# Four score-table units ahead of the sort products, and half of the keyed one-hot rows made by ScalarE

## The reference, cut to what matters

```python
x1 = x[edges[0]]
x2 = x[edges[1]]
e = jnp.concatenate([x1, x2], axis=1) @ Ww + bw          # 12288 x 1024
e = e.reshape(-1, H, 2 * HD).transpose(1, 0, 2)
e = jax.nn.leaky_relu(e, 0.01)
w = (e @ Wa + ba)[..., 0]
mat = jnp.full((H, n, n), -jnp.inf, jnp.float32)
mat = mat.at[:, edges[0], edges[1]].set(w)
mat = jnp.nan_to_num(jax.nn.softmax(mat, axis=-1))
y = jnp.matmul(mat, out).transpose(1, 0, 2)
```

## Time and profile before

| | us |
|---|---|
| three runs | 1829.89, 1833.54, 1833.86 |
| their median | 1833.54 |
| the profiled execution | 1831.71 |
| its span, from the first to the last instruction | 1829.8 |

### The profile page before, as it was taken

The page is one execution under the profiler, slowest core; times in us unless marked ns, Lnnn a source line. Parts: engine busy times, 40 slices in busy tenths (PEclk is TensorE's granted clock), DMA queues, the critical chain, the costliest instruction groups (busy, mean ns, idle before and its releaser), DMA issues.

```text
span 1829.8 us, 22981 instructions
## 1 busy us (share of the span) xinstructions
PE 1593.3 (87%) x7110; PEld 879.4 (48%) x7111; DVE 920.3 (50%) x2224; ACT 501.2 (27%) x1607; POOL 521.8 (29%) x548
## 2 busy tenths in 40 slices
PE   5989999997697999999993396769699899999698
PEld 3534444445444646455552273624244455555455
DVE  8888888887644343443443035988732101011322
ACT  1134444447421414132230112511210211111233
POOL 5843333333332332222233721637500000000000
PEclk9999999998798999999996597679899999999899
DMA  7030101005424233232213472656525222210020
GB/s 307 6 102 20 57 24 59 24 8 131 121 56 129 63 88 79 59 105 56 70 47 93 117 259 70 176 145 185 166 69 189 69 75 69 97 53 28 8 62 18
DMA packets 132571, 162.74 MB, mean 89 GB/s; under 512 B 62041, under 2 KB 74601, under 8 KB 132114
## 3 DMA queue, kind: packets, MB, share of 16 engines
q1 hardware_dynamic: 105888, 116.45, 20.6%
q0 software_dynamic: 18752, 29.91, 6.3%
q10 hardware_dynamic: 7858, 15.44, 2.6%
HBM read 145.87 MB, written 15.88 MB: 88 GB/s over the span
## 4 chain that ended last, share of the span: by engine, by line
PE 64%; DMA 16%; DVE 12%; issue 5%; ACT 2%; POOL 1%; DVEq 0%; ACTq 0%; POOLq 0%; SPq 0%
PE psum L377 62%; DMA tab_sorted<-rec,pos 12%; DVE arena L2572 2%; DMA tab_w<-xT,pair 1%; DVE ring L1329 1%; DVE stats L468 1%; DMA ring<-tab_h,sd_t 1%; DVE ring L1264 1%; PE psum L1008 1%; DMA arena<-tab_h,sd_t 0%; PE psum L2231 0%; DMA arena<-tab_w 0%; DVE arena L1332 0%; DVE arena L1238 0%; DVE ring L1236 0%
## 5 line engine op out<-in xcount | busy, mean ns | idle before, releaser
L377 PE MATMUL psum<-arena 128*128 128x24 bf16 (+8 forms) x2026 | 324.0, 317 | 30.2 <-DVE arena L654 12.9
L377 PE MATMUL psum<-arena,ring 128*128 (+1 forms) x1504 | 327.3, 364 | 8.8 <-issue 6.3
L377 PE MATMUL psum<-xT,ring 128*128 128x384 f32 x928 | 318.6, 505 | 10.0 <-ACT ring L3006 4.2
L377 PE MATMUL psum<-ring,arena 128*128 128x512 f32 (+1 forms) x592 | 271.4, 605 | 8.7 <-DVE ring L654 3.9
L377 PEld LDWEIGHTS psum<-arena 128*128 128x128 bf16 (+5 forms) x2026 | 198.6, 149 | 162.0 <-issue 74.1
L377 PE MATMUL psum<-ring,xT 128*128 128x512 f32 x552 | 251.1, 607 | 2.5 <-DMA bc<-in_wide 1.4
L377 PEld LDWEIGHTS psum<-xT,ring 128*128 128x128 f32 x928 | 182.1, 198 | 140.2 <-issue 29.1
L377 PEld LDWEIGHTS psum<-arena,ring 128*128 128x128 bf16 (+1 forms) x1504 | 140.2, 115 | 127.4 <-issue 28.4
L1059 ACT ACTIVATE ring<-ring 128x128 f32<-128x128 f32 x416 | 123.3, 298 | 179.8 <-DVE ring L1329 179.8
L2114 POOL DMA_INDIRECT tab_sorted<-rec,pos x104 | 100.0, 961 | 237.2 <-DMA tab_sorted<-rec,pos 224.6
L377 PEld LDWEIGHTS psum<-ring,arena 128*128 128x128 f32 (+1 forms) x592 | 102.6, 187 | 135.3 <-issue 134.2
(11 more groups left out here) (455 smaller groups left out, 1600.1 us busy)
## 6 DMA issues: line engine op xcount, KB each, us to landing
ring<-in_L_ffn_w SPq DMA_DIRECT2D x22, 1024.0 KB, 8.0
ring<-in_L_gnn_m_w SPq DMA_DIRECT2D x8, 1024.0 KB, 5.9
ring<-in_L_ffn_expert_weights SPq DMA_DIRECT2D x8, 1024.0 KB, 5.3
ring<-tab_key ACTq DMA_DIRECT2D x24, 256.0 KB, 3.2
ring<-in_L_gnn_Wv SPq DMA_DIRECT2D x5, 1024.0 KB, 5.1
tab_w<-xn SPq DMA_DIRECT2D x6, 768.0 KB, 15.1
ring<-in_L_gnn_Ww SPq DMA_DIRECT2D x4, 1024.0 KB, 17.3
ring<-in_L_gnn_wq SPq DMA_DIRECT2D x4, 1024.0 KB, 5.6
```

What stands on the lines that cost most here:

```text
L377: return nc.tensor.matmul(o, a, b, start=start, stop=stop)
```

## The change

`EARLY` becomes 4, so units 0 to 3 stand ahead of the first group, and `AFTER_GROUP` gives out units 4 to 9 after groups 2, 4, 5, 7, 8 and 10, so that none follows group 11. Of the eight keyed rows of a group, ScalarE makes the first four in two activations each: the distance from the place, `abs(r - n)`, into a new tile `apart`, and `relu(key - key * distance)` into `spread`, which is the key where the distance is 0 and nothing elsewhere. VectorE makes the other four and the eighth column one-hot as before, and one new small instruction for the negated keys. TensorE waits for ScalarE's half too (`act_spread`). ScalarE's unit parts are now placed after the groups by the list that VectorE has. The gathers of the third block use eight `rows_landed` semaphores of their own.

```diff
-        rows_landed = sems("rows_landed", GR - UN) + ranks_landed
+        rows_landed = sems("rows_landed", UN)
...
         def row_landed(eng, T):
-            earlier = 1 if T % GR < 2 * NT else RECORDS + ST // UN if T % GR >= GR - UN else 0
-            eng.wait_ge(rows_landed[T % GR], 16 * (earlier + T // GR + 1))
+            earlier = 1 if T % UN < 2 * NT else 0
+            eng.wait_ge(rows_landed[T % UN], 16 * (earlier + T // UN + 1))
...
+        ACT_SPREADS = UN // 2
+        key_less = cs_e
+        apart = view(e0, 2, ACT_SPREADS, P)
...
-        EARLY = 2
-        AFTER_GROUP = {1: 2, 2: 3, 4: 4, 5: 5, 7: 6, 8: 7, 10: 8, 11: 9}
+        EARLY = 4
+        AFTER_GROUP = {2: 4, 4: 5, 5: 6, 7: 7, 8: 8, 10: 9}
         SPLIT_AFTER = {0: 0, 1: 1, 3: 2, 4: 3, 6: 4, 7: 5, 9: 6, 10: 7, 11: 8}
...
-            unit(0)
-            unit(1)
+            for u in range(EARLY):
+                unit(u)
...
                 pe.wait_ge(spread_made, g + 1)
+                pe.wait_ge(act_spread, g + 1)
...
             top_part(0)
-            for u in range(len(UNITS)):
+            act.wait_ge(keys_ready, 1)
+            for g in range(ET // UN):
+                if g >= 2:
+                    act.wait_ge(sort_used, g - 1)
+                for j in range(ACT_SPREADS):
+                    t = UN * g + j
+                    last = nc.scalar.activation(apart[:, g % 2, j, :], iota[:, 0:P], ACT.Abs, bias=r_f[:, t:t + 1], scale=-1.0)
+                last.then_inc(apart_made, 1)
+                act.wait_ge(apart_made, g + 1)
+                for j in range(ACT_SPREADS):
+                    t = UN * g + j
+                    last = nc.scalar.activation(spread[:, g % 2, j, :], apart[:, g % 2, j, :], ACT.Relu, bias=slo1[:, t:t + 1],
+                                                scale=key_less[:, t:t + 1])
+                last.then_inc(act_spread, 1)
+                if g in SPLIT_AFTER:
+                    middle_part(SPLIT_AFTER[g])
+            for u in range(len(SPLIT_AFTER), len(UNITS)):
+                middle_part(u)
...
+            V.tensor_scalar(key_less, slo1, -1.0, None, ALU.mult).then_inc(keys_ready, 1)
...
-                    last = V.tensor_scalar(spread[:, g % 2, j, :], iota[:, 0:P], r_f[:, t:t + 1], slo1[:, t:t + 1],
-                                           ALU.is_equal, ALU.mult)
+                    if j >= ACT_SPREADS:
+                        last = V.tensor_scalar(spread[:, g % 2, j, :], iota[:, 0:P], r_f[:, t:t + 1], slo1[:, t:t + 1],
+                                               ALU.is_equal, ALU.mult)
```

More of the change, by code:

```diff
@@ L266, in gnn_ffn_program @@
         spread_made = sem("spread_made")
+        apart_made = sem("apart_made")
+        act_spread = sem("act_spread")
         sort_used = sem("sort_used")
@@ L276, in gnn_ffn_program @@
         hote_made = sem("hote_made")
+        keys_ready = sem("keys_ready")
         z_full = sem("z_full")
@@ L638, in pool_scatter_rows @@
                     row_landed(pool, T - ROWS_UNDERWAY)
-                pool_gather(go_rows[T % GR], table, sd_t[:, T:T + 1]).then_inc(rows_landed[T % GR], 16)
+                pool_gather(go_rows[T % GR], table, sd_t[:, T:T + 1]).then_inc(rows_landed[T % UN], 16)
         def dve_scatter_rows(dve, od):
@@ L1039, in top_part, with middle_part @@
                 nc.scalar.activation(unit_part(u, 0), b, ACT.Copy).then_inc(hi_made, 1)
-            top_part(0)
-            for u in range(len(UNITS)):
+            def middle_part(u):
                 if u + 1 < len(UNITS):
@@ L1046, in _ @@
                 nc.scalar.activation(unit_part(u, 1), left_f[:, u % 2, :], ACT.Copy).then_inc(bf16_made, 1)
+            top_part(0)
+            act.wait_ge(keys_ready, 1)
[16 more added lines that the diff above has]
+                middle_part(u)
             act.wait_ge(sorted_cleared, 16)
@@ L1262, in _ @@
                     if j >= POOLED:
-                        V.tensor_scalar(slot_one[:, g % 2, j, :], iota[:, 0:P], q_f[:, t:t + 1], None, ALU.is_equal)
-                    last = V.tensor_scalar(spread[:, g % 2, j, :], iota[:, 0:P], r_f[:, t:t + 1], slo1[:, t:t + 1],
-                                           ALU.is_equal, ALU.mult)
+                        last = V.tensor_scalar(slot_one[:, g % 2, j, :], iota[:, 0:P], q_f[:, t:t + 1], None, ALU.is_equal)
+                    if j >= ACT_SPREADS:
+                        last = V.tensor_scalar(spread[:, g % 2, j, :], iota[:, 0:P], r_f[:, t:t + 1], slo1[:, t:t + 1],
+                                               ALU.is_equal, ALU.mult)
                 last.then_inc(spread_made, 1)
```

## The result

The changed kernel takes 1836.62 us (median of 22 runs, 1831.33 to 1842.01), the kernel before 1830.57 us in 22 runs beside them (1825.07 to 1838.0): a ratio of 1.003, interval 1.0019 to 1.004. It is 0.3% slower, where "no difference" was forecast. The profiled execution of the changed kernel is the 1842.01 us one, with a span of 1840.3 us; the pair of traces is 10.5 us apart, the medians 6.05 us. So the traces show where time goes, and the ratios how much it usually is.

What follows compares the result with a forecast made beforehand. TensorE was taken to bound the stage's second half, so unit 11's end counted: 97.4 or 99.4 us against 98.4, middle 0.0, hence 1833.5 us beside the runs' median of 1833.54. The range ran from 1829 to 1838.

Steps and rivals of the forecast that it cites:

- B: Sort stage: GpSimd isn't late, its rows get quicker as VectorE sheds work; -4.5 us, 1829.0 us; chance 8%.
- C: Sort stage: ScalarE becomes the maker TensorE waits for; unit 11 7.3 us later, 1840.8 us; chance 10%.
- I take the middle, 0.0: End of unit 11: between -1.0 and +1.0 us against 98.4 us, the change was put at 0.0.
- Case D: Sort stage: exchange of waits with slow GpSimd groups and low clock behind the keys; +2.7 us, 1836.2 us; chance 22%.
- the low clock behind the keys: Units 10 and 11: the wait for the keys might lower TensorE's clock, costing 1.7 us, at even chances.
- the slow bound of 4.25 to 4.90: GpSimd's one-hots in groups 2 to 4: 4.25 or 4.90 us a group, the slow value being 4.90.
- healing: GpSimd's slow groups: half the row work on VectorE might make them quicker; nothing showed whether it would.
- hidden, but for 0.4 us: Group 2: a low clock of 3.41 us would be covered by the 1.3 us wait for group 4.
- the 99.4 of the bad end: End of unit 11 with GpSimd's slow groups: 99.4 us, +1.0 us against 98.4.
- It has slack to catch up: GpSimd's record and weight scatters: starting 1 to 3 us later costs nothing, given 19 waits of 35.6 us in all.
- those 1 to 3 us: GpSimd's scatters: the cost if it had no slack to catch up after its later group 11.
- an exchange of waits: Sort stage, the main forecast: old waits go, new ones come; -1.0 to +1.0 us, 1833.5 us; chance 60%.

Runs made afterwards that it cites:

- run 3: The kernel before with only the eight own semaphores for the gathers of the third block: 1887.21 us, ratio 1.001.
- run 4: The changed kernel as it is, profiled a second time, against the kernel before: 1888.4 us, ratio 1.0025.
- run 5: The kernel before with only the new order of units (four early); VectorE makes all eight keyed rows: 1893.2 us, ratio 1.0039.
- run 2: The kernel before with unit 11 computed twice on TensorE, GpSimd's order untouched: 1888.93 us, ratio 1.003.
- run 8: As run 6, with GpSimd making five of a group's column one-hots instead of seven and VectorE three; against the kernel before: 1887.63 us, ratio 1.0013.
- run 9: The kernel before with 24 instead of 20 record scatters ahead of the weight scatters: 1884.91 us, ratio 0.9971.
- run 10: The kernel before without GpSimd's one-hots in the last two groups and with 24 record scatters ahead: 1893.9 us, ratio 1.003.
- run 6: The changed kernel with the old unit order, ScalarE's rows kept and its unit parts moved; against the kernel before: 1887.39 us, ratio 1.0001.
- run 11: run 8 without GpSimd's one-hots in the last two groups and with 26 record scatters ahead; against the kernel before: 1892.05 us, ratio 1.0025.
- run 1: The kernel before with seven unused one-hots chained on GpSimd behind its last group: 1893.08 us, ratio 1.005.
- run 12: run 8 with 24 instead of 20 record scatters ahead; against the kernel before: 1834.51 us, ratio 0.9995.
- run 7: The kernel before with the 76 late record scatters issued between the weight scatters: 1893.77 us, ratio 1.0029.

## Why the prediction was wrong

**What held.** TensorE went to group 0 at 34.9 us (34.4 forecast), the wait of 1.80 us went, GpSimd became the late maker with a standstill of 5.2 us, and the keys cost 2.2 us (2.4) once unit 9 no longer covered them. ScalarE's group is 2.9 us for 3.0 forecast, no table was loaded, VectorE and ScalarE were late for no group: rivals B and C are out. No cost of the semaphores shows (run 3). The Trainium skill, "ScalarE: Activation LUTs", section "What ACT_TABLE_LOAD costs", would have given ScalarE's price closer than my rows of other shapes: a start of 186 ns with 0.833 ns a column, 93 ns for each operand that is a column of SBUF, 93 ns of overlap. Worked out for 128 columns, as an estimate, that is 1.26 us for four Abs and 1.64 us for four Relu. The trace agrees, 1.27 and 1.65 us.

**The step that failed first: "I take the middle, 0.0".** Case D, the exchange with the bad ends, is what happened, and I had given it 22%. It moved unit 11 by 4.2 us (3.7 in run 4), and D said 2.7. That D's 1836.2 us and the measured 1836.62 almost agree is luck: the forecast stood on three runs with a median of 1833.54, and over 22 the kernel before has 1830.57, so D's +2.7 met a measured +6.05. The middle of -1.0 and +1.0 also left out the low clock behind the keys, 1.7 us at even chances. By the sum's own terms:

- GpSimd's group took 4.92 us, at the slow bound of 4.25 to 4.90, in the first trace of the change, and no less in run 4 and in run 5 with VectorE making all rows. (Without group 5, which the prediction averaged in, groups 2 to 4 took 5.06 us each before.) The slow groups aren't caused by the amount of row work on VectorE, so "healing" was no possibility. The rows give the cause. In the timeline of VectorE the low part of a unit (`split_unit`, line 1246 here, both operands in SBUF) is under way, and in the timeline of GpSimd the two one-hots beside it take 2.18 us instead of 1.19:

```profile
44.39 0.67 DVE L1246 TENSOR_TENSOR arena<-ring,arena 128x512 bf16<-128x512 f32 x1
```

```profile
43.36 2.18 POOL L1165 TENSOR_SCALAR ring<-iota,xT 128x128 f32<-128x128 f32 x2
```

The line by itself has 592 ns at least and 1544 ns at most, before 593 and 1642. The other slow one, 1.28 us, stands beside the 128x832 product of `tile_chunks`. The seven others over 0.9 us in this trace have such a low part beside them too, for a shorter time. `tile_chunks` and these parts run in groups 2 to 4 whatever VectorE sheds.

```profile
L1165 POOL TENSOR_SCALAR ring<-iota,xT x84: 592/597/1544, 22.9 to 85.0; 128x128 f32<-128x128 f32 x84
```

The Trainium skill, "GPSIMD Engine Reference", section "1. Specifications", says the same: GpSimd shares its SBUF interface with VectorE and they contend when a VectorE instruction has two SBUF inputs. I hadn't used it.

- The low clock at group 2 was to be "hidden, but for 0.4 us", by a wait of 1.3 us ahead of group 4. It lasted 6.8 us in place of 3.41, swallowed that wait, and put group 4 at 52.06 us, 0.9 later than the 51.15 of the slow groups; 0.5 of that is the later start.
- From there to the end of group 11 took 37.0 us for 36.2.
- The low clock behind the keys, put at even chances, came in both traces of the change (unit 10 in 5.29 us) and not in run 5 (3.60 us). It is 1.7 us, as sized.

51.15 to 52.06 is 0.9, then 0.8, then 0.2 less for the keys and 1.7 for the clock: 3.2 us on top of the 99.4 of the bad end, 102.6.

**The second step: "It has slack to catch up".** I read it off, 19 waits for VectorE's result and 35.6 us in all. The same row in the changed kernel, in the trace where GpSimd is 5.4 us later at the end, is no smaller:

```profile
  DMA tab_w<-xT,pair: 163.1, 79
  DVE xT L1371: 39.2, 20
```

So that sum of waits doesn't tell what GpSimd can give back. The lags tell more. From tile 10 to 33 they stand at one of three levels, about 1, 4 or 7 us, a tile's 2.9 us apart. Those at 1 us (runs 2, 3, 8, 9 and 10) or at 4 us (the kernel before, runs 4, 5, 6 and 11) end at 8.8 or 9.1 us; those at 7 us (the first trace of the change, runs 1 and 12) end at 14.2 us. From the first two levels the end is the same, so the 3 us between them are given back, and that far the step holds. From the third it fails, and a delay of a few us costs 5.4 us at the end. A falling lag by itself is no proof of catching up, since it also falls when the tiles come late: in run 9 the 3.8 us between tiles 0 and 15 are the 3.9 that the loop lost. The prediction priced GpSimd's delay at nothing, and at "those 1 to 3 us" if there were no slack; its first record scatter was 5.1 us later, and it had no term for a level, nor for late signals in the loop. A late unit 11 is another matter. It moves the tiles themselves, and run 2 shows all of it at the end, as the prediction had it.

**In sum.** The mechanism of the stage (an exchange of waits, GpSimd next) was right and its sum stood at the wrong end: 3.7 to 4.2 us, nearly each term at its bad bound or past it. The lag adds nothing or 5.4 us, a held loop up to 1. That is some 4 to 10 us, and the measured 0.3%, 5.5 us, lies between. The first failed step alone comes to 0.20 to 0.23% and is shown; how the rest splits between lag and held loop over the 22 runs, two traces don't show. Run 5 has the whole loss with the new order alone (1.0039, unit 11 at 101.0 us), run 6 has none with ScalarE's rows alone (1.0001, unit 11 at 97.8 us); their intervals are half a per cent wide, so it is the traces that separate the two.

**Open.** What puts the lag at 4 or at 7 us (at tile 0 it was 2.6 us in both traces of the change, 4.4 in run 9 and 3.9 in run 12); why TensorE's signals came 5 to 20 us late in runs 10 and 11, and 0.7 to 3.9 us late in runs 1, 4, 5, 7 and 9; and how much of run 9's gain comes from the records, since its own trace accounts for 0.6 us at the long wait.

## What to carry to other kernels

The waits of an engine for its producer, summed, don't measure its slack: subtract the two timelines, here the scatter's start and its tile's score, and see at which distance it runs and whether it comes back. Then look at both timelines by themselves too, because the distance also shrinks when the producer falls behind, as in run 9. When an edit takes work from the engine that a wait names, look first who is next: here GpSimd had been ready only 0.9 us before VectorE. And where several terms of a sum are open, ask whether they share a cause: the slow one-hots, the longer wait and the low clock behind it came together, and the middle of the sum was none of the cases.

## What the runs showed of the hardware

- A one-hot of 128x128 on GpSimd takes 0.60 us, and up to 1.54 us (before 1.64) beside VectorE instructions with two operands in SBUF; a group of seven, some 4.2 us else, takes 4.9 us on the average of groups 2 to 4 by it (5.1 before).
- A wait of 3.35 us was followed by a granted clock of 0.50 for 6.8 us in one trace and for a shorter time in another of the same kernel; a wait of 2.82 us by 3.41 us of it, one of 2.68 us in run 3 by none, one of 1.99 us in runs 3 and 9 by 3.4 us; the stand of 2.21 us behind group 11 by 3.4 us in two traces and by none in a third.
- GpSimd's single indirect scatters, each waiting for the one before, go every 2.83 us in the weight stage: 0.96 us to issue and 1.87 us of idle time until the one before has landed. Their lag behind the tiles stood at levels about 3 us apart and rose near scatters 34 and 67 in every trace, wherever it had begun; only in run 7 did it come back each time.
- With 24 and 26 record scatters issued in an unbroken row, ScalarE and VectorE took TensorE's results 5 to 20 us late, in two kernels; in five others VectorE took them 0.7 to 3.9 us late in the tile loop, in one of them 17 times, with record scatters between the weight scatters, and not once for the 25 tiles behind the last of these. 0.04 us is usual. The cause is open.
- On the chips of runs 1 to 11 the part behind the long wait took 833 to 850 us, on the others 794 to 797, and in the one pair on the same sort of chip the changed kernel has 794.6 us for 793.5.
